# Row-by-row loads of one edge tile in five steps of sixteen, and window loads from byte offsets, in a three-layer graph network

## What is computed

```python
h = node_features @ enc_W + enc_b
for l in range(3):
    cat = jnp.concatenate([h[src], h[dst], edge_features], axis=-1)
    m = jax.nn.relu(cat @ msg_W1[l] + msg_b1[l]) @ msg_W2[l] + msg_b2[l]
    agg = jax.ops.segment_sum(m, dst, num_segments=n_nodes)
    h = gru_cell(agg, h, gru_Wih[l], gru_Whh[l], gru_bih[l], gru_bhh[l])
out = jax.nn.relu(h @ ro_W1 + ro_b1) @ ro_W2 + ro_b2
return layernorm(x + out)
```

## Time and profile before

| | |
|---|---|
| median of 3 runs | 9798.1 us (9768.75 to 9832.15) |
| the profiled execution, its own time | 9777.42 us |
| its span, first to last instruction | 9775.6 us |
| granted TensorE clock, mean | 0.571 |
| busy: PE, VectorE, ACT, POOL | 2880.1, 3532.6, 346.4, 4639.2 us |
| rows of `p_src` loaded one by one | 9792 from SP, 9792 from ACT |
| gathers | 4830 |

### The profile page before, as it was taken

One profiled execution on the slowest core, in us unless ns is written; L12 is line 12 of the kernel. 1 busy time (PEld: TensorE's weight loads), 2 busy tenths in 40 slices (PEclk: granted clock), 3 DMA queues, 4 the chain that ended last, 5 costly groups with the idle time before them and its releaser, 6 DMA issues.

```text
span 9775.6 us, 72182 instructions
## 1 busy us (share of the span) xinstructions
PE 2880.1 (29%) x7290; PEld 1610.2 (16%) x7290; DVE 3532.6 (36%) x4656; ACT 346.4 (4%) x542; POOL 4639.2 (47%) x4865
## 2 busy tenths in 40 slices
PE   3323322322322332222222222223232222322223
PEld 2111111111111221111111111112111111111112
DVE  2333333333333433333333333333333334333334
ACT  0000000000000000000000000000000000000001
POOL 5444444444444454444444444445454445545543
PEclk6555555555555555555555555555555555555555
DMA  3111111111111111111111111111111111111111
GB/s 87 31 31 30 30 30 30 28 31 30 31 30 30 30 28 30 30 30 30 30 30 29 30 30 27 30 31 30 30 31 31 30 30 34 31 31 31 31 30 25
DMA packets 351443, 308.63 MB, mean 32 GB/s; under 512 B 149364, under 2 KB 237518, under 8 KB 350568
## 3 DMA queue, kind: packets, MB, share of 16 engines
q0 software_dynamic: 155328, 159.79, 8.6%
q1 hardware_dynamic: 118271, 110.17, 4.0%
q10 hardware_dynamic: 77328, 33.96, 1.4%
HBM read 280.52 MB, written 22.83 MB: 31 GB/s over the span
## 4 chain that ended last, share of the span: by engine, by line
SPq 57%; issue 38%; DVE 2%; PE 1%; another core or an unknown queue 1%; DMA 0%; ACT 0%; POOL 0%; DVEq 0%; ACTq 0%; POOLq 0%
SPq L473 46%; SPq L469 6%; SPq L642 2%; SPq L633 1%; SPq L527 1%; DVE work_ps L1493 1%; SPq L630 1%; DVE folds L1528 0%; DVE p_src L1490 0%; PE bank L838 0%; DMA p_src<-p_tab 0%; PE work_ps L949 0%; PE bank L962 0%; SPq L662 0%
## 5 line engine op out<-in xcount | busy, mean ns | idle before, releaser
L798 POOL DMA_INDIRECT p_src<-p_tab,idx_all x4767 | 4551.1, 955 | 4916.8 <-DVE work_ps L1493 3467.4
L962 PE MATMUL bank<-hot,folds 128*128 128x96 f32 x2496 | 660.1, 413 | 4012.9 <-issue 2053.0
L1490 DVE TENSOR_TENSOR p_src<-work_ps,p_src 128x512 f32<-128x512 f32 x624 | 427.6, 685 | 3374.9 <-DMA p_src<-p_tab 2912.1
L962 PEld LDWEIGHTS bank<-hot,folds 128*128 128x128 f32 x2496 | 532.1, 296 | 4278.5 <-issue 2198.0
L949 PE MATMUL work_ps<-w_edges,msg 128*128 128x512 f32 x1248 | 1120.0, 997 | 21.4 <-DMA windows_sb<-q_tab 21.4
L1523 DVE SCALAR_TENSOR_TENSOR work_ps<-work_ps,rel 128x1024 f32<-128x1024 f32 x624 | 768.8, 1232 | 21.5
L1493 DVE TENSOR_TENSOR work_ps<-p_src,bank 128x1024 f32<-128x1024 f32 x624 | 767.0, 1229 | 21.4
L1528 DVE TENSOR_REDUCE folds<-work_ps 128x256 f32<-128x1024 f32 x624 | 758.4, 1215 | 0.0
L959 PE MATMUL bank<-hot,counts 128*34 128x96 bf16 x416 | 68.9, 261 | 2248.6 <-issue 1278.6
L1538 DVE TENSOR_TENSOR sums<-bank,sums 128x96 f32 x624 | 158.1, 253 | 872.6 <-remote 699.5
L959 PEld LDWEIGHTS bank<-hot,counts 128*34 128x34 bf16 x416 | 27.1, 108 | 2368.2 <-issue 1359.8
(11 more groups left out here) (167 smaller groups left out, 1800.9 us busy)
## 6 DMA issues: line engine op xcount, KB each, us to landing
p_src<-p_tab ACTq DMA_DIRECT2D x9792, 0.2 KB
p_src<-p_tab SPq DMA_DIRECT2D x9792, 0.2 KB
p_src<-p_tab,idx_all POOLq DMA_INDIRECT x4830
msg<-in_edge_k SPq DMA_DIRECT2D x156, 256.0 KB
pick<-rel_tab SPq DMA_DIRECT2D x312, 96.0 KB
windows_sb<-q_tab ACTq DMA_DIRECT2D x312, 24.0 KB
windows_sb<-q_tab SPq DMA_DIRECT2D x312, 24.0 KB
pick<-q_tab ACTq DMA_DIRECT2D x312, 24.0 KB
```

The source lines that it names most:

```text
L798: pool.indirect_dma_start(out=p_src[r][0:rows, t, :], out_offset=None, in_=p_tab[l][0:NODES, :], in_offset=bass.IndirectOffsetOnAxis(ap=id ...
L962: last = nc.tensor.matmul(fold_ps, folds[:, b, :], hot_all[n % 2][:, s * BLOCKS + b, 1:WINDOW + 1], start=(b == 0), stop=(b == BLOCKS - 1))
L1490: nc.vector.tensor_tensor(rows, edge_ps[k % 2], rows, ALU.add).then_inc(with_edge, 1)
```

## The change

- Layer 0 keeps one tile row by row in each of the steps 3, 7, 11, 15 of sixteen (51 steps). Layers 1 and 2 now have it in 3, 6, 9, 12, 15 of sixteen (64 steps each), so 179 such steps in place of 153. Each still has 64 rows from SP and 64 from ACT.
- The pieces of 16 rows get a due time in fifths of a step: piece q of step m at `max(5 * m - 25 + every * q, 0)`, with `every` 5 in layer 0 and 4 in layers 1 and 2. ACT issues at step m those due in `[5m, 5m + 5)`, SP ahead of group g those due in the four steps that begin at 4g - 10. In layer 0 this gives the old order on both queues.
- The windows are addressed in bytes. `spread` and `late`, free by then, are overwritten by VectorE with `256 * base` and `256 * (base + 22)`; SP and ACT read these, so that the multiplication of each start (a FUSED_REGOPS ahead of each window load) falls away. The bytes moved are the same.
- `src_single` and `offsets` now have 90 rows in place of 52.

```diff
-AHEAD_OF = 5
-SINGLES = GROUPS - 1
+SINGLE_STEPS = [[m for m in range(STEPS - 1) if m % 16 in kinds] for kinds in ((3, 7, 11, 15), (3, 6, 9, 12, 15), (3, 6, 9, 12, 15))]
+SINGLE_ROWS = sorted(set(SINGLE_STEPS[0] + SINGLE_STEPS[1]))
+SINGLES = len(SINGLE_ROWS)
...
+        first_bytes = [spread[:].bitcast(I32), late[:].bitcast(I32)]
...
-        def has_singles(m):
+        def has_singles(l, m):

-            return m % GROUP == GROUP - 1 and m // GROUP < SINGLES
+            return m in SINGLE_STEPS[l]
...
-                here = offsets[m // GROUP:m // GROUP + 1, at:at + PIECE]
+                here = offsets[SINGLE_ROWS.index(m):SINGLE_ROWS.index(m) + 1, at:at + PIECE]
...
-        def pieces_at(m):
-
-            due = [(m + AHEAD_OF - q, q) for q in range(PIECES)]
-            if m == 0:
-                due = [(GROUP - 1, q) for q in range(PIECES) if GROUP - 1 + q <= AHEAD_OF]
-            return [(at, q) for at, q in due if at < STEPS and has_singles(at)]
+        def pieces_between(l, a, b):
+
+            every = 5 if len(SINGLE_STEPS[l]) < STEPS // 4 else 4
+            return [(m, q) for m in SINGLE_STEPS[l] for q in range(PIECES) if a <= max(5 * m - 25 + every * q, 0) < b]
...
+        def group_starts(kind, g, b):
+
+            return nc.values_load_multi_w_load_instructions(
+                first_bytes[b][0:1, GROUP * g:GROUP * (g + 1)], engines=(kind,), min_val=b * AHEAD * ROW_BYTES, max_val=(NODES + b * AHEAD) * ROW_BYTES,
+                skip_runtime_bounds_check_because="base_i is a destination, at most NODES, and a row is as long as the factor")[1]
+
+        def window_rows(l, start):
+
+            here = q_tab[l].bitcast(U8).rearrange("n b -> (n b)")[bass.ds(start, ROW_BYTES)]
+            return bass.AP(here.tensor, here.offset, [[ROW_BYTES, REACH], [1, 2 * ROW_BYTES]])
...
-                bases = group_bases(sp, mybir.EngineType.SP, g)
+                starts = group_starts(mybir.EngineType.SP, g, 0)
                 for j in range(GROUP):
-                    here = q_tab[l][bass.ds(bases[j], REACH), :]
-                    pairs = bass.AP(here.tensor, here.offset, [[HID, REACH], [1, PAIR]])
-                    sp.dma_start(windows_of[GROUP * (n % 2) + j][0:REACH, 0:PAIR], pairs).then_inc(edges_in[n % 2], 16)
+                    sp.dma_start(windows_of[GROUP * (n % 2) + j][0:REACH, 0:PAIR].bitcast(U8), window_rows(l, starts[j])).then_inc(edges_in[n % 2], 16)
...
-                        single_rows(sp, mybir.EngineType.SP, l, GROUP * (g - 2) + GROUP - 1, 0, SP_ROWS, sp_singles)
+                        for m, q in pieces_between(l, 0 if g == 2 else 5 * (GROUP * (g - 1) - 6), 5 * (GROUP * g - 6)):
+                            single_rows(sp, mybir.EngineType.SP, l, m, PIECE * q, PIECE, sp_singles)
                         group_inputs(n0 + g, g)
                         group_windows(l, n0 + g, g)
...
-                        for at, q in pieces_at(m):
+                        for at, q in pieces_between(l, 5 * m, 5 * m + 5):
                             single_rows(act, mybir.EngineType.Activation, l, at, SP_ROWS + q * PIECE, PIECE, act_singles)
...
+                for b in range(2):
+                    nc.vector.tensor_scalar(first_bytes[b], base_i[:], float(ROW_BYTES), float(b * AHEAD * ROW_BYTES), ALU.mult, ALU.add)
```

More of the change, by code:

```diff
@@ L191, in build @@
         both = pre_all[:].rearrange("p s g f -> p (s g f)")
-        raw_nodes = zr[0:GROUPS, 0:128].bitcast(I32)
-        offsets = p_src[ROW_SLOTS].rearrange("p t f -> p (t f)")[0:GROUPS, 0:128].bitcast(I32)
+        raw_nodes = zr[0:SINGLES, 0:128].bitcast(I32)
+        offsets = p_src[ROW_SLOTS].rearrange("p t f -> p (t f)")[0:SINGLES, 0:128].bitcast(I32)
         src_seen = [dst_flat[:, 0:STEP], both[0:LATE_ROWS, :].bitcast(I32)]
@@ L451, in build, with gathers_of @@
         late_ps = [zr_ps[:], n_ps[:]]
-        def gathers_of(m):
-            return LAST_TILES if m == STEPS - 1 else EDGE_TILES - has_singles(m)
-        def has_singles(m):
-            return m % GROUP == GROUP - 1 and m // GROUP < SINGLES
+        def gathers_of(l, m):
+            return LAST_TILES if m == STEPS - 1 else EDGE_TILES - has_singles(l, m)
+        def has_singles(l, m):
+            return m in SINGLE_STEPS[l]
         def single_rows(eng, kind, l, m, first, n, landed):
@@ L474, in single_rows @@
                                   table[bass.ds(start, ROW_BYTES)].unsqueeze(0)).then_inc(landed[nth_single(l, m) % SINGLE_SEMS], 16)
-        def pieces_at(m):
-            due = [(m + AHEAD_OF - q, q) for q in range(PIECES)]
-            if m == 0:
-                due = [(GROUP - 1, q) for q in range(PIECES) if GROUP - 1 + q <= AHEAD_OF]
-            return [(at, q) for at, q in due if at < STEPS and has_singles(at)]
+        def pieces_between(l, a, b):
+            every = 5 if len(SINGLE_STEPS[l]) < STEPS // 4 else 4
+            return [(m, q) for m in SINGLE_STEPS[l] for q in range(PIECES) if a <= max(5 * m - 25 + every * q, 0) < b]
         def nth_single(l, m):
-            return l * SINGLES + m // GROUP
+            return sum(len(SINGLE_STEPS[j]) for j in range(l)) + SINGLE_STEPS[l].index(m)
         def chunk_stages(m):
@@ L693, in _ @@
                             chunk_nodes(g // 2 + 1)
-                    single_rows(sp, mybir.EngineType.SP, l, STEPS - 1 - GROUP, 0, SP_ROWS, sp_singles)
+                    for m, q in pieces_between(l, 5 * (GROUP * (GROUPS - 1) - 6), 5 * STEPS):
+                        single_rows(sp, mybir.EngineType.SP, l, m, PIECE * q, PIECE, sp_singles)
                     if l == 0:
@@ L749, in _ @@
             for m in range(PRE):
-                for t in range(gathers_of(m)):
+                for t in range(gathers_of(0, m)):
                     pool.indirect_dma_start(
@@ L787, in _ @@
                         if early(l, m):
-                            for t in range(gathers_of(m)):
+                            for t in range(gathers_of(l, m)):
                                 pool.indirect_dma_start(
@@ L802, in _ @@
                 for m in range(PRE):
-                    pool.wait_ge(ahead[m], 16 * gathers_of(m))
+                    pool.wait_ge(ahead[m], 16 * gathers_of(0, m))
                 pool.wait_ge(idx_first_in, 16)
@@ L1181, in windows_ahead @@
             def windows_ahead(l, n, g):
-                bases = group_bases(act, mybir.EngineType.Activation, g)
+                starts = group_starts(mybir.EngineType.Activation, g, 1)
                 for j in range(GROUP):
-                    here = q_tab[l][bass.ds(bases[j] + AHEAD, REACH), :]
-                    pairs = bass.AP(here.tensor, here.offset, [[HID, REACH], [1, PAIR]])
-                    act.dma_start(windows_of[GROUP * (n % 2) + j][REACH:ROWS, PAIR:2 * PAIR], pairs).then_inc(ahead_in[n % 2], 16)
+                    act.dma_start(windows_of[GROUP * (n % 2) + j][REACH:ROWS, PAIR:2 * PAIR].bitcast(U8), window_rows(l, starts[j])).then_inc(ahead_in[n % 2], 16)
             with act.If(slow == 0):
@@ L1473, in landed @@
             def landed(k):
-                return 16 * sum(gathers_of(j % STEPS) for j in range(k % ROW_SLOTS, k + 1, ROW_SLOTS) if j >= PRE)
+                return 16 * sum(gathers_of(j // STEPS, j % STEPS) for j in range(k % ROW_SLOTS, k + 1, ROW_SLOTS) if j >= PRE)
             def edge_sums(k):
@@ L1481, in edge_sums @@
                 if k < PRE:
-                    dve.wait_ge(ahead[k], 16 * gathers_of(k))
+                    dve.wait_ge(ahead[k], 16 * gathers_of(0, k))
                 else:
                     dve.wait_ge(gathered[r], landed(k))
-                if has_singles(k % STEPS):
+                if has_singles(k // STEPS, k % STEPS):
                     n = nth_single(k // STEPS, k % STEPS)
@@ L1698 @@
         "src": src.transpose(2, 0, 1, 3).reshape(128, STEPS, EDGE_TILES),
-        "src_single": src[GROUP - 1::GROUP, BLOCKS - 1, :, RUN - 1],
+        "src_single": src[SINGLE_ROWS, BLOCKS - 1, :, RUN - 1],
         "src_early": src[0:EARLY].transpose(0, 1, 3, 2).reshape(EARLY, STEP),
```

## The result

The changed kernel takes 10,372.1 us (median of 4 runs, 10,357.0 to 10,378.7) against 9799.7 us for the kernel before in the same set of runs: a ratio of 1.059, 95% interval 1.0566 to 1.0615. It is slower, as forecast, by 572 us; the forecast was 10,260 us, which is 460 above that median. The profiled execution took 10,378.7 us, its span is 10,376.9 us, and the mean granted clock 0.565 (0.571 before).

A forecast was written before the change was run, and what follows sets the result against it. SP's queue, issuing single rows, was taken as the bound. Onto the profiled 9777.4 us came +234 (layer 1), +250 (layer 2), -17 (layer 0), together +467, and some 15 for waits and starts: 10,260 us, range 10,060 to 10,450.

The forecast's parts named there:

- What bounds the kernel: SP's queue, issuing single rows and reads of their offsets, holds 57% of the span; DMA engines are busy 4.0%.
- 13 more singles, +334 us a layer: SP's queue, layers 1 and 2: 64 singles in place of 51, 25.7 us each, nothing hidden, +334 us each.
- Shorter bursts, -52 us a layer: POOL's gathers, layers 1 and 2: 64 bursts where 51 were, each giving SP back 4.0 us, -52 us each.
- the toll: SP's queue while POOL gathers: a burst of n gathers costs 1.19 n - 4 us; 33.0 of a cycle's 62.6.
- Extra breaks: POOL's bursts, VectorE held at the node update: 6 extra in layer 1, which had 2; 33 kept in layer 2.
- Windows, -17 us a layer: SP's window loads: the dropped multiplication saves some 0.08 us each, -17 us a layer; new load form taken at 0.32 us.
- The 15 us added for waits and starts: Some 15 us added to the sum for reads of offsets with a wait and starts of layers, not placed.
- Dealt pieces, setup, ACT: 0: SP's new waits for `joined` and `mixed`, setup ahead of the layers, and ACT's 13 more singles: each taken as 0.
- B: SP's queue: added rows are hidden in idle SP time, no change, about 9,700 us; chance 0.02.
- C: ACT, between sigmoid and tanh: its added pieces make it last, +260 us, 10,520 us; chance 0.09.
- D: SP's queue under gathers: toll is 1.06 (layer 1) and 0.98 us (layer 2) a gather, about 10,380 us; chance 0.18.
- A: SP's queue under gathers: shorter bursts stop the toll, 9,380 us; decides from 285 bursts in two layers; chance 0.03.

The follow-up runs named there:

- the repeat of the kernel before: The kernel before, unchanged, executed once more in a later set with the toll: 9789.4 us, a single execution.
- the second pair: The kernel before and the changed kernel, both unchanged, run again with the toll: 9789.4 and 10,367.8 us against 9818.2; ratio of the changed kernel 1.0554.

## Why the prediction was right, and where it was off

The measured 10,372 us lie inside the stated range, and the queue that was named is the one that costs the time. Part of the nearness is luck, as the terms below show.

*What bounds the kernel.* Right: SP's queue, whose work is issue and not bytes. Shown three ways. The chain of the changed kernel is the same; layer 0 without single rows, SP's and ACT's, is 801 us shorter; and pauses that load POOL and leave the rows of both queues as they are take 543 us off layer 2, where SP's queue leads the chain.

*13 more singles, +334 us a layer.* Right in size. The price of 25.7 us is met in the open: 64 rows take 25.02 us by the timeline, and a read ahead of them. Were it hidden, layer 1 could not have grown by 252 us.

*Shorter bursts, -52 us a layer.* Right in direction and near in size: the toll of both changed layers is within 13 us of what this form gives for the bursts that are there, in both executions. It isn't exact: in the repeat of the kernel before it gives 1663 us for layer 2 (57 bursts), and 1591 are measured, as pauses just under 4.5 us help too and the form doesn't count them. That the same gathers cost SP less in more bursts is shown by the breaks in layer 2. They gave 6.1 us each, more than the 4.0 that was taken from two timelines of before: so what a burst gives back is not a constant, and bursts of 8 and 15 give back more each than bursts of 23 and 31.

*Extra breaks.* This is the step that failed: "and leave at 33 in layer 2". The changed kernel has 65 bursts there, one extra. The 32 that are missing are worth 32 x 4.0 = 128 us by my price, and layer 2 came out 371 - 250 = 121 us longer than I said. That the two agree so well is in part luck: in the second pair the layer grew by 322, a miss of 72, because that execution of the kernel before had few extra bursts itself. In both executions of the changed kernel they are gone (65 and 67, against 64 from the singles alone). I had the numbers to see it. The earlier trace rows put the pause after the 23rd gather, and the text gave 23 gathers as the length of the new bursts: a pause that comes after three buffers can't be an extra one when the burst ends after three. In layer 1 I counted on 70 bursts and 66 came, 16 of the 18 us by which that layer was missed.

*Windows, -17 us a layer.* The sign is right and the size too large. From the end of the last load of relative rows to the end of the fourth window load SP takes a median of 2.55 us before and 2.36 after, so 0.19 us a group and some 10 us a layer. The FUSED_REGOPS are gone, but the load's own issue has a median of 0.364 us, where I took the old 0.32. The 15 us of layer 0 arise elsewhere. SP's first single row starts at 123.7 in place of 140.7, since the eight window loads ahead of it, which stand under POOL's first gathers, take 2.8 and 5.7 us where they took 6.4 and 13.5; how much of that is the new form of load isn't shown. From there to the last single row of the layer it is 3198 us, where it was 3195, and in the second pair 3188 and 3173. In those stretches SP waited longer for VectorE at the shift counts, so they neither show nor exclude 10 us. With the toll no run measures the windows by themselves.

*The 15 us added for waits and starts* have no row behind them, and no run shows them. What lies between and behind the layers came out 7 us shorter.

*Dealt pieces, setup, ACT: 0.* Right for the first, by SP's 13.5 us for `joined` and 29.2 for `mixed`. ACT was not last in any of the 179 steps, and "its cover is thin" is measured now: one more piece in every second single, and ACT's queue leads the chain, with the toll and without it. Its tanh is waited for 430 us, where it was 381.

*The rivals.* B and C did not occur. D, no term for bursts, gave 10,380 and came within 10 us of the result, but for another reason: by D layer 1 would have grown by some 300 us (it grew by 252), and the breaks in layer 2 could have brought nothing. A, short bursts stop the toll, had the right mechanism and price; the changed kernel makes 131 bursts in the two layers, far from the 285 at which it decides. The kernel with breaks added has 154 in layer 2, over the 2.2 a cycle, and that layer takes 2900 us, less than the 3072 before the change.

*What I did not foresee* is that the toll comes and goes with the same kernel. Its whole price of some 3620 us was on the page as a cost of this kernel, and both forecast and rivals hold only in its presence.

## What to carry to other kernels

Where the chain lies on a queue and "issue" while the DMA engines are at 4%, count instructions of that queue, not bytes: price one piece in the open and one beside the other engines' load, and expect any added piece to cost in full. Where such a queue slows under another engine's long bursts, short pauses in the bursts can be worth more than they cost (here 541 us of pauses bought 543 us net), and a change of period should be checked for pauses that fall together. Before tuning against such a slowdown, measure the same kernel more than once, some time apart: with these runs a version can be 7% faster in one state and 13% slower in the other, and the changed kernel is slower by 5.5 to 5.9% in one and, without its window part, faster by 0.4% in the other.

## What the runs showed of the hardware

- The same program takes 6154 or some 9800 us. In the long kind a MOVE and a DMA issue of SP slow down from some 4 us after a burst of indirect DMAs begins, until each takes 0.7 us and starts 1.4 us after the one before: a row every 0.32 us becomes a row every 2.8 us, from 16 us on, and it is 0.32 again 2 us after the burst. In the short kind they take 0.029 and 0.228 us under the gathers too. What puts the chip into the one or the other is open: the kind held for all executions of a set, was tied to no kernel, and changed on one chip within ten minutes.
- A read of 14 or 18 offsets into registers takes 1.2 to 4.8 us, against 1.23 for 16 of them from a multiple of 16.
- 128 rows of 256 bytes by indirect DMA take 1.26 us of POOL, one after the other.

Open as well: no kernel without singles in all layers was seen with the toll. Layer 0 alone, 801 us shorter, suggests that dropping them everywhere would be the larger gain there, and without the toll it costs 3.1%. The changed kernel itself was not run without the toll, only its two parts.
